# Two-stage transformer block, 64 tiles: the scalar chain between attention and MLP, done in two halves of 32 tiles inside the neighbouring slots

## The reference

```python
def logmap0(x): n = _norm(x); return arctanh(clip(n, EPS, MAX_TANH_ARG)) * x / n
def expmap0(v): n = _norm(v); return tanh(n) * v / n
def mobius_add(x, y):            # x2, y2, xy: row sums of x*x, y*y, x*y
    return ((1+2*xy+y2)*x + (1-x2)*y) / (1 + 2*xy + x2*y2).clip(EPS)
def plin(x, w, b): return expmap0(logmap0(x) @ w + b)

sh_msa, sc_msa, g_msa, sh_mlp, sc_mlp, g_mlp = split(t_emb @ w_ada + b_ada, 6)
xm = expmap0(layer_norm(logmap0(x)) * (1 + sc_msa) + sh_msa)
attn_out = attention(xm)                          # 16 heads of 16 channels
x  = mobius_add(x, expmap0(g_msa * logmap0(attn_out)))
xm = expmap0(layer_norm(logmap0(x)) * (1 + sc_mlp) + sh_mlp)
ff = plin(plin(xm, w_f1, b_f1), w_f2, b_f2)
return input + mobius_add(x, expmap0(g_mlp * logmap0(ff)))
```

## Time and profile before

| | |
|---|---|
| median of 3 runs | 885.65 us (885.09 to 887.93) |
| the profiled execution | 887.88 us, of it the span from first to last instruction 886.1 us |
| TensorE busy | 723.1 us (82%) |
| VectorE busy | 687.9 us (78%) |
| ScalarE busy | 554.0 us (63%) |
| GpSimd busy | 405.5 us (46%) |
| mean granted TensorE clock | 0.946 of full speed |

### The profile page before, as it was taken

How to read it: one execution, slowest core, us unless ns; L and a number is a source line. 1 busy time by engine, 2 the same in 40 slices (tenths; PEclk the granted TensorE clock), 3 DMA queues, 4 the chain that set the end, 5 groups by cost and what they waited for, 6 DMA issues and landing times.

```text
span 886.1 us, 30432 instructions
## 1 busy us (share of the span) xinstructions
PE 723.1 (82%) x9409; PEld 523.8 (59%) x9423; DVE 687.9 (78%) x2243; ACT 554.0 (63%) x1504; POOL 405.5 (46%) x806
## 2 busy tenths in 40 slices
PE   0945899898989999998989899704779999979987
PEld 0644677777777777777777777502335555545556
DVE  1686888888888888888888887465989998968971
ACT  0103677777777777777777777524757666747651
POOL 2001655555555555555555555201246555635644
PEclk9977999999999999999999999656899999989999
DMA  9911111111111111111111110022334544434422
GB/s 310 349 65 54 50 55 53 53 46 53 48 51 51 53 53 53 53 53 53 48 52 47 51 51 21 20 60 60 107 107 121 138 136 144 134 100 142 129 69 84
DMA packets 51656, 74.82 MB, mean 84 GB/s; under 512 B 7176, under 2 KB 34192, under 8 KB 51600
## 3 DMA queue, kind: packets, MB, share of 16 engines
q1 hardware_dynamic: 48768, 70.41, 26.5%
q10 hardware_dynamic: 2576, 3.28, 1.1%
q0 software_dynamic: 256, 0.53, 0.2%
HBM read 65.02 MB, written 9.18 MB: 84 GB/s over the span
## 4 chain that ended last, share of the span: by engine, by line
PE 43%; DVE 23%; issue 18%; POOL 5%; DMA 4%; ACT 3%; DVEq 2%; SPq 0%; ACTq 0%; POOLq 0%
PE p_qkv L829 20%; PE p_oz L803 8%; DVE u L1083 7%; PE p_s L819 3%; DVE g_all L1118 2%; DMA g_all<-in_L_cond_b_f 2%; PE p_s L892 2%; PE p_oz L797 2%; DVEq L50 1%; DVE arrays L977 1%; PE p_qkv L892 1%; DVE qk L1158 1%; PE p_o L903 1%; DMA mod<-mod_rows 1%; PE p_o L905 1%
## 5 line engine op out<-in xcount | busy, mean ns | idle before, releaser
L829 PE MATMUL p_qkv<-wqkv,tT 128*128 128x256 f32 x768 | 194.4, 390 | 30.4 <-DVE u L1083 30.1
L829 PEld LDWEIGHTS p_qkv<-wqkv,tT 128*128 128x128 f32 x768 | 134.9, 191 | 61.5 <-DVE u L1083 21.9
L453 POOL TENSOR_TENSOR qk<-qk 128x512 f16<-128x512 f32 x64 | 74.1, 1157 | 145.6 <-ACT qk L567 145.6
L843 PEld LDWEIGHTS p_o<-v,pT 64*64 64x64 f32 x4096 | 68.9, 137 | 36.2 <-issue 36.2
L1111 DVE TENSOR_TENSOR z<-p_oz,bo 128x256 f32<-128x256 f32 x64 | 27.2, 425 | 78.3 <-PE p_oz L803 78.2
L572 ACT ACTIVATE qkT<-p_s 128x1024 f32<-128x1024 f32 x64 | 65.6, 1025 | 33.1 <-PE p_s L786 33.1
L843 PE MATMUL p_o<-v,pT 64*64 64x17 f32 x4096 | 73.4, 210 | 12.1 <-ACT pT L617 12.1
L617 ACT ACTIVATE pT<-p_s 128x1024 f32<-128x1024 f32 x64 | 65.5, 1024 | 20.5 <-PE p_s L819 20.5
L803 PE MATMUL p_oz<-wo,oT 128*128 128x256 f32 x256 | 75.2, 418 | 0.6 <-ACT oT L577 0.5
L1083 DVE SCALAR_TENSOR_TENSOR u<-p_qkv,ct,bqkv 128x768 f32<-128x768 f32 x64 | 65.1, 1017 | 12.1 <-issue 9.3
L786 PE MATMUL p_s<-ident,qk 128*128 128x128 f16 x1024 | 68.7, 221 | 6.5 <-issue 4.2
(11 more groups left out here) (247 smaller groups left out, 1766.7 us busy)
## 6 DMA issues: line engine op xcount, KB each, us to landing
mod<-mod_rows SPq DMA_DIRECT2D x128, 128.0 KB, 2.8
x_all<-in_x SPq DMA_DIRECT2D x8, 1024.0 KB, 14.4
gate<-mod_rows SPq DMA_DIRECT2D x128, 64.0 KB, 2.5
mod<-mod_rows SPq DMA_DIRECT2D x32, 256.0 KB, 4.0
mod_b<-mod_rows SPq DMA_DIRECT2D x32, 256.0 KB, 3.9
out<-x_all SPq DMA_DIRECT2D x32, 256.0 KB, 2.2
gate<-gate_rows SPq DMA_DIRECT2D x32, 128.0 KB, 2.9
bqkv<-gate_rows SPq DMA_DIRECT2D x32, 128.0 KB, 3.4
```

Of the source, the lines that this page charges most:

```text
L453: pool.tensor_tensor(low, qk[:, :].rearrange("p (a h d) -> p a h d", a=2, d=HD), qk4[:, :, :, 0, :], ALU.subtract).then_inc(low_ready, 1)
L829: mm = pe.matmul(p_qkv[:, a * D:a * D + D], tT[:, k, c, :], wqkv[:, c, a * D:a * D + D], start=c == 0, stop=c == C - 1)
L843: mm = pe.matmul(p_o[S * e:S * e + S, col:col + VW], pT[keys, e, g, :], v[keys, k, 2 * g + e, :], start=True, stop=True, skip_group_check= ...
```

## The change

The scalar chain is cut into nine functions (`norm_of_z`, `clip_of_z`, `gated_norm`, `sum_factors`, `sum_moments`, `sum_norm`, `log_map_argument` with `log_map_series`, `log_map_norm`, `scale_of_norm`) that work on the columns `cols[0]`, 32 of 64. The pieces of tiles 0 to 31 stand in VectorE's attention slots 60 to 69, ahead of `add_bo`, with ScalarE's functions at the ends of those slots. Those of tiles 32 to 63 stand in MLP slots 0 to 7, behind `shift_t2`; their first one is ahead of slot 0. The order of steps in a half is that of before, but for the series, which now comes ahead of the wait for the logarithm. The attention loop ends at slot 60 (`LAST`) and no longer at 64, so that slots 60 to 63 are written out. The first half's end signals `factors_made`, for which the MLP waits; ScalarE waits for the second in MLP slot 15. `stage_done` is signalled and nobody waits for it.

```diff
+        cols = [slice(0, T)]
+
         def row(k):
-            return arrays[:, k, :]
+            return arrays[:, k, cols[0]]
...
+        LAST = T - 4
...
         def run_tiles(eng, slot):
-            run_slots(eng, slot, FIRST, T, T + L_L)
+            run_slots(eng, slot, FIRST, LAST, T + L_L)
...
+                for s in (LAST, LAST + 1, LAST + 5, LAST + 8):
+                    if at_slot(h, off, s):
+                        rsq()
+                if at_slot(h, off, LAST + 2):
+                    elementwise(ACT.Tanh, W7, W8)
+                    act.preload_act_table_set("natural_log_exp_and_others")
+                if at_slot(h, off, LAST + 7):
+                    elementwise(ACT.Ln, W7, W8)
+
+            cols[0] = slice(0, HALF)
             run_tiles(act, slot)
-
-            rsq()
-            rsq()
-            elementwise(ACT.Tanh, W7, W8)
-            act.preload_act_table_set("natural_log_exp_and_others")
-            rsq()
-            elementwise(ACT.Ln, W7, W8)
-            rsq()
...
                     for j in range(2):
                         scale_x(slots - M_A, j)
+                if at_slot(h, off, 0, TURN):
+                    rsq()
...
                         square_t2(slots - M_A, j, (off - M_A) % 2)
+                for s in (0, 4, 6):
+                    if at_slot(h, off, s, TURN):
+                        rsq()
+                if at_slot(h, off, 1, TURN):
+                    elementwise(ACT.Tanh, W7, W8)
+                    act.preload_act_table_set("natural_log_exp_and_others")
+                if at_slot(h, off, 5, TURN):
+                    elementwise(ACT.Ln, W7, W8)
...
-
-            act.preload_act_table(ACT.Tanh)
+                if at_slot(h, off, 6, TURN):
+                    act.preload_act_table(ACT.Tanh)
+                if at_slot(h, off, 2 * TURN - 1, TURN):
+                    act.wait_ge(factors_made, 2)
+
             act.wait_ge(factors_made, 1)
+            cols[0] = slice(HALF, T)
             run_pairs(act, slot2)
...
+            def norm_of_z():
+
+                dve.wait_ge(stats_kept, cols[0].stop)
+                step(dve.tensor_scalar(row(W0), sm(0), EPS2, None, ALU.max))
+                put()
+
+            def clip_of_z():
+
+                take_rsq(W4)
+                ts(W4, W4, AM, ALU.mult, 1.0, ALU.min)
+                tt(W5, W4, W4, ALU.mult)
+                add(W0, row(W5), sm(3), ALU.mult)
+                ts(W0, W0, EPS2, ALU.max)
+                put()
+
+            def gated_norm():
+
+                take_rsq(W6)
+                tt(W7, W0, W6, ALU.mult)
+                put()
+
+            def sum_factors():
+
+                answered()
+                tt(W8, W8, W6, ALU.mult)
...
+            def scale_of_norm():
+
+                take_rsq(W4)
+                tt(R2, W12, W4, ALU.mult)
+                dve.drain().then_inc(factors_made, 1)
...
                     sum_rows(2 * h + off - L_D)
+                if at_slot(h, off, LAST):
+                    norm_of_z()
+                if at_slot(h, off, LAST + 1):
+                    clip_of_z()
+                if at_slot(h, off, LAST + 2):
+                    gated_norm()
+                if at_slot(h, off, LAST + 3):
+                    sum_factors()
+                if at_slot(h, off, LAST + 4):
+                    sum_moments()
+                if at_slot(h, off, LAST + 5):
+                    sum_norm()
+                if at_slot(h, off, LAST + 7):
+                    log_map_argument()
+                    log_map_series()
+                if at_slot(h, off, LAST + 8):
+                    log_map_norm()
+                if at_slot(h, off, LAST + 9):
+                    scale_of_norm()
...
+                if at_slot(h, off, 0, TURN):
+                    clip_of_z()
+                if at_slot(h, off, 1, TURN):
+                    gated_norm()
+                if at_slot(h, off, 2, TURN):
+                    sum_factors()
+                if at_slot(h, off, 3, TURN):
+                    sum_moments()
+                if at_slot(h, off, 4, TURN):
+                    sum_norm()
+                if at_slot(h, off, 5, TURN):
+                    log_map_argument()
+                    log_map_series()
+                if at_slot(h, off, 6, TURN):
+                    log_map_norm()
+                if at_slot(h, off, 7, TURN):
+                    scale_of_norm()
...
+            norm_of_z()
             run_pairs(dve, slot2)
```

More of the change, by code:

```diff
@@ L286, in build, with run_slots, at_slot @@
         FIN_STEPS = 15
-        def run_slots(eng, slot, first, items, slots):
+        def run_slots(eng, slot, first, last, slots):
             for s in range(first):
                 slot(s // 2, s % 2)
-            with eng.Fori(first // 2, items // 2) as h:
+            with eng.Fori(first // 2, last // 2) as h:
                 slot(h, 0)
                 slot(h, 1)
-            for s in range(items, slots):
+            for s in range(last, slots):
                 slot(s // 2, s % 2)
+        def at_slot(h, off, s, per_turn=2):
+            return isinstance(h, int) and per_turn * h + off == s
         def count(n):
@@ new lines, in gated_norm @@
+            def gated_norm():
+                take_rsq(W6)
+                tt(W7, W0, W6, ALU.mult)
+                put()
+            def sum_factors():
+                answered()
+                tt(W8, W8, W6, ALU.mult)
+                tt(W9, W8, W4, ALU.mult)
+                tt(W10, W9, W9, ALU.mult)
+                add(W10, row(W10), sm(3), ALU.mult)
+                add(W11, row(W9), sm(2), ALU.mult)
+                ts(W11, W11, 2.0, ALU.mult, 1.0, ALU.add)
+                tt(W12, XX, W10, ALU.mult)
+                tt(W12, W12, W11, ALU.add)
+                ts(W12, W12, EPS, ALU.max)
+                step(dve.reciprocal(row(W12), row(W12)))
+                tt(W13, W11, W10, ALU.add)
+                tt(ALPHA, W13, W12, ALU.mult)
+                tt(W13, OMX, W9, ALU.mult)
+                tt(BETA, W13, W12, ALU.mult)
@@ new lines, in sum_moments @@
+            def sum_moments():
+                step(dve.tensor_scalar(row(W9), sm(1), 1.0 / D, None, ALU.mult))
+                tt(W10, W9, W9, ALU.mult)
+                step(dve.scalar_tensor_tensor(out=row(W10), in0=sm(3), scalar=1.0 / D, in1=row(W10), op0=ALU.mult, op1=ALU.subtract))
+                tt(W11, W9, MEAN, ALU.mult)
+                step(dve.scalar_tensor_tensor(out=row(W11), in0=sm(2), scalar=1.0 / D, in1=row(W11), op0=ALU.mult, op1=ALU.subtract))
+                tt(W12, ALPHA, MEAN, ALU.mult)
+                tt(W13, BETA, W9, ALU.mult)
+                tt(MEAN1, W12, W13, ALU.add)
+                tt(W12, ALPHA, ALPHA, ALU.mult)
+                tt(W13, ALPHA, BETA, ALU.mult)
+                tt(W14, BETA, BETA, ALU.mult)
+                tt(W9, W12, VAR, ALU.mult)
@@ new lines, in log_map_argument, with log_map_series @@
+            def log_map_argument():
+                take_rsq(W4)
+                tt(W5, W0, W4, ALU.mult)
+                ts(W5, W5, MAX_ARG, ALU.min)
+                ts(W6, W5, -1.0, ALU.mult, 1.0, ALU.add)
+                step(dve.reciprocal(row(W6), row(W6)))
+                stt(W7, W5, 1.0, W6, ALU.add, ALU.mult)
+                put()
+            def log_map_series():
+                tt(W9, W5, W5, ALU.mult)
+                ts(W10, W9, 1.0 / 15, ALU.mult)
+                for m in (13, 11, 9, 7, 5, 3):
+                    stt(W10, W10, 1.0 / m, W9, ALU.add, ALU.mult)
+                ts(W10, W10, 1.0, ALU.add)
+                tt(W10, W10, W5, ALU.mult)
+                tt(W10, W10, W4, ALU.mult)
+                ts(W11, W5, SERIES_BELOW, ALU.is_lt)
@@ L1240, in _ @@
[L1240 to L1249 removed]
+            dve.drain().then_inc(stage_done, 1)
```

67 lines of the change are left out of this document (35 added, 32 removed).

## The result

Median of four executions 892.68 us (891.61 to 894.47), against 886.57 us (885.09 to 887.93) of the kernel before beside it: ratio 1.0077, 95% interval 1.0057 to 1.0098. The change makes the kernel 0.8% slower, where 885.1 us and "no change" were forecast and 891 us was the end of the range. The profiled execution took 894.47 us, its span is 892.7 us, 6.6 us more than before.

The account below looks back on a forecast made before the run. Attention was taken as bound by a VectorE-TensorE ring, the first MLP slots by a nearly full VectorE. Terms -25.4 + 2.3 + 8.0 - 0.7 + 13.8 + 1.5 = -0.5 us gave 885.1 us; range 878.5 to 891.

Parts of the forecast that it names:

- (a): Between attention and MLP: the gap before the first `first_sum` goes; gain 25.4 us.
- (b): MLP start: first `mod` loads, no longer covered by the chain, delay `scale_t2`; cost 2.3 us, bounds 0 and 3.8.
- (c): Price of one chain step on 32 columns: 0.225 us, bounds 0.20 and 0.257; 82 steps per half, about 18.7 us.
- (d): Attention slots 60 to 69: first half's pieces overrun VectorE's wait for `z`; cost 8.0 us, slot 63 worst at 4.2.
- The Tanh loads: End of slot 62: two table loads and Tanh on ScalarE delay `usq` in slot 63; 2.1 us.
- three signs: Steps not near 0.225 us; slot 63 not over 10; first eight MLP slots growing under 12 or over 20 us.
- Unroll: Slots 60 to 63 leave the loop: two jumps of 0.38 us less, -0.7 us.
- (e): MLP slots 0 to 7: second half's pieces in VectorE's nearly full queue; cost 13.8 us, bounds 10 and 17.6.
- (f): Slots 63 to 65, MLP 3 to 8: holes in TensorE's work may lower its clock; 1.5 us, bounds 0 and 7.
- rival A: TensorE goes slow in slots 63 to 66; clock term becomes 5 to 7 us, total about 889.5; chance 0.25.
- B: Faster: pieces hide better in the MLP and in slot 63; total about 879.5 us; chance 0.25.
- C: MLP start stays tied to something else, as a later `mod` transfer or the gates; about 889 us; chance 0.06.

Follow-up runs that it names:

- experiment 6: Changed kernel with first half's steps spread over more slots, Tanh's load back put off, first `mod` rows requested early: 876.06 us, kernel before 885.86, ratio 0.9896.
- experiment 1: Changed kernel with GpSimd's `low_parts` in slots 60 to 68 cut to 16 of 512 columns: 887.37 us, kernel before 886.34, ratio 1.0012.
- experiment 3: Changed kernel with the first half's Tanh replaced by Exp, so without the two table loads: 890.53 us, kernel before 886.34, ratio 1.0049.
- experiment 9: Kernel before with only attention slots 60 to 63 written out: 878.92 us, kernel before 885.43, ratio 0.9929.
- 2: Kernel before with `low_parts` cut in slots 60 to 68 and slots 60 to 63 written out: 879.32 us, kernel before 886.34, ratio 0.9932.
- experiment 7: Changed kernel with the first half's chain run between the stages, only the second half moved: 892.42 us, kernel before 885.86, ratio 1.0085.
- experiment 8: Changed kernel with filler transposes on TensorE in slots 66 to 69: 888.46 us, kernel before 885.86, ratio 1.0038.
- experiment 10: Changed kernel with at most three steps a slot in slots 49 to 63, written out from 48, early `mod` rows: 869.20 us, before 885.43, ratio 0.9835.

## Why the prediction was wrong

**(a), (b) right.** The gap gave 25.5 us for 25.4, and the transfer cost 2.8 for 2.3; experiment 6 takes it back.

**(c) right.** 0.18 to 0.21 us a step, spaced 0.22.

**(d) the step that failed.** The sum of the overruns was right against the profile that it started from: with `low_parts` out of the way slots 61 to 69 grow by 8.2 us (experiment 1), where 8.8 was forecast with the clock. That it came so near is in part luck: the drain of that profile was slow already, and slots 66 and 68 were off in opposite directions. The Tanh loads cost 2.16 for 2.1 (experiment 3); the extra 1.38 us beside each load, which the prediction quotes and does not count, do not show (two loads and the function in 2.84 us). Wrong was the sentence "All pieces stand between `sum_rows` and `add_bo`, that is in the wait for `z`", as the place where a step costs 0.225 us and no more. VectorE's wait was free of VectorE's work, not of GpSimd's: `low_parts` lies there in every slot, and one instruction of VectorE stood still for the rest of it, six times, 5.25 us. The price of a step was taken from the border, where GpSimd is idle (the busy time before PEclk is GpSimd's, 0.00 us), and carried to a place where it is not.

```profile
580.00:600.00 20.00, 0.00 (x0) 0.00 (x0) 15.38 (x66) 4.34 (x9) 0.00 (x0) 0.50 0.27 64
```

That is most of the 7.1 us between forecast and profile.

The Trainium skill has the rule, on its page "SBUF — State Buffer", section "Who interferes with whom": a VectorE instruction with two inputs in SBUF and a GpSimd instruction that reads SBUF share a port, and the second to issue waits until the first is done. The rows agree: 1.18 us for a step of 0.19 beside GpSimd's 1.17. That `tensor_scalar` can take the shared port too (same section) fits the row at 560.03, 1.02 us for 0.19. The prediction did not ask what GpSimd does in the wait. None of the three signs by which it would have called itself wrong (the step, slot 63, the MLP's first slots) could show this, and none of them came up.

**Unroll, -0.7.** Mis-sized: alone it measures -6.3 us (4.3 to 8.2). The slots give 1.4 of it, the clock little, and the rest is unexplained. In the change none of it beyond the jumps shows; its profile has the drain at 1.2 GHz, and the mean clocks of its other executions (0.944 to 0.946) say the same of them. Against experiment 9 as its base the change costs 13 us, by the two ratios, and even with the stall taken out 8 us (experiment 1 against 2). So the forecast of no change rested on a base that could be had 6 us faster without the split.

**(e) right within 1 us**: 14.6 for 13.8, and 14.3 by itself in experiment 7 (15.6 against experiment 9, whose own first MLP slots were 1.3 us shorter). No wait for `p_qkv` was left in MLP slots 4 and 6. It was overlooked that VectorE's queue there is no cheaper than the border: a half costs in the MLP 14.3 us, and the whole chain on its own some 25.

**(f) and rival A.** Half right. The forecast took the profiled execution as its base, whose drain was already at 0.51, and so put 1.5 us for the clock. What A described happened (a hole of 3.8 us in slot 63, 1.2 GHz behind it), and fillers in slots 66 to 69 give 2.2 us back in those slots (experiment 8), though slots 64 and 65 took 0.6 us more there. But A's price of 5 to 7 us was too high on the forecast's base: with the stall gone, and the clock down as before (0.946 to 0.948 in all executions of experiment 1), nothing is left over beyond the 1.5 us. The clock was not the larger cause. What the change would take with TensorE at 2.4 GHz throughout wasn't run. The price of slot 66, +1.28 us where nothing was forecast, is part of it: with fillers slot 66 takes 5.39 us. B and C did not occur.

What stays open: why TensorE keeps its clock in one execution and loses it in the next behind the same holes, what makes the first MLP slots differ by up to 2.5 us between profiles with one MLP code, and where some 4.5 us of the gain of writing out come from.

## What to carry to other kernels

A wait of one engine is free only if what you put in it shares nothing with what the others do in that time: look up all engines' rows in the window, not just the waiting one's. Split a serial chain by steps that end before the neighbour begins (three steps cost nothing here, a fourth or fifth that met GpSimd's instruction 1.0 to 1.35 us), not by halves that double the count of steps whose price hardly falls with their width. Before an edit of the structure around the change is booked at the price of its jumps, time it alone, and take the result as the base for the rest: experiment 9 has 6 of experiment 10's 15 to 16 us without a split. Profile the kernel before more than once.

## What the runs showed of the hardware

- A VectorE instruction with two SBUF inputs that began behind a GpSimd `tensor_tensor` of 1.16 us lasted until that had ended: 0.19 us became 1.18, 0.47 became 1.41. So did a `tensor_scalar`, 1.02 for 0.19. A reduction beside it kept its 0.95, and a `z` with one input in PSUM its 0.43.
- With TensorE holes equal within 0.01 us, the granted clock in the drain was 0.51 in one execution of a kernel (560 to 579) and 1.00 in another (560 to 575); slots 61 to 69 took 63.70 and 58.59 us, and the execution as a whole 887.88 and 885.07.
- Fp32 steps of 128 partitions, each waiting for its own end: 0.20 us at 8 columns, 0.22 at 32, 0.257 at 64. Halving a chain's columns took 3.4 us of 27.7.
